# Sixteen 4 MB loads and sixteen 4 MB stores: two DMA queues, or one queue in a fixed order

## The reference

```python
W = weights[condition]                       # 64 x 128 x 128
return x + jnp.einsum('bct,bcd->bdt', x, W)  # 64 x 128 x 2048
```

## Time and profile before

| | us |
|---|---|
| median of 3 runs | 320.15 (319.94 to 320.36) |
| the profiled execution's own time | 320.04 |
| its span, first to last instruction | 318.3 |
| TensorE busy | 246.5 (77%) |
| VectorE busy | 146.8 (46%) |
| bytes moved | 135.29 MB, 425 GB/s over the span |

### The profile page before, as it was taken

The page is one execution under the profiler, slowest core; times in us unless marked ns, Lnnn a source line. Parts: engine busy times, 40 slices in busy tenths (PEclk is TensorE's granted clock), DMA queues, the critical chain, the costliest instruction groups (busy, mean ns, idle before and its releaser), DMA issues.

```text
span 318.3 us, 1351 instructions
## 1 busy us (share of the span) xinstructions
PE 246.5 (77%) x512; PEld 104.6 (33%) x512; DVE 146.8 (46%) x65; POOL 18.9 (6%) x69
## 2 busy tenths in 40 slices
PE   0099999991996979779398895939979596796960
PEld 0044444440442424334143342414424242342420
DVE  0026766762252553735237362641626556055460
POOL 0000000000010000001000010000000001000000
PEclk9999999998796998999779799996979999598996
DMA  8999999999999999999999999999999999999997
GB/s 329 416 441 457 371 424 457 397 461 399 457 424 432 449 408 461 412 445 432 424 453 404 457 424 432 445 412 461 399 457 424 432 449 408 461 395 461 420 411 298
DMA packets 5187, 135.29 MB, mean 425 GB/s; under 512 B 578, under 2 KB 578, under 8 KB 578
## 3 DMA queue, kind: packets, MB, share of 16 engines
q1 hardware_dynamic: 2448, 68.16, 50.0%
q10 hardware_dynamic: 2738, 67.11, 48.9%
HBM read 68.16 MB, written 67.11 MB: 425 GB/s over the span
## 4 chain that ended last, share of the span: by engine, by line
DMA 61%; PE 33%; DVE 3%; issue 0%; SPq 0%
PE product L92 33%; DMA out<-x_ring 32%; DMA x_ring<-x 30%; DVE x_ring L108 3%; SPq L58 0%
## 5 line engine op out<-in xcount | busy, mean ns | idle before, releaser
L92 PE MATMUL product<-x_ring,chosen_weights 128*128 128x512 f32 x512 | 246.5, 644 | 61.4 <-DMA x_ring<-x 61.4
L108 DVE TENSOR_TENSOR x_ring<-product,x_ring 128x2048 f32<-128x2048 f32 x64 | 146.7, 2291 | 161.4 <-PE product L92 161.4
L92 PEld LDWEIGHTS product<-x_ring,chosen_weights 128*128 128x128 f32 x512 | 104.6, 207 | 202.4 <-issue 122.7
L80 POOL COPY chosen_weights<-weight_table 128x128 f32 x64 | 18.7, 293 | 284.6 <-DVE x_ring L108 277.7
L102 DVE TENSOR_SCALAR state_row<-condition_row 1x64 int32<-1x64 int32 x1 | 0.2, 182 | 2.0 <-DMA condition_row<-condition 2.0
L137 POOL MEMSET const-float32-0.0<- 128x1 f32 x1 | 0.1, 98 | 0.1
L137 POOL MEMSET const-bfloat16-1.0<- 128x1 bf16 x1 | 0.1, 101 | 0.0
L137 POOL MEMSET const-uint8-127<- 128x1 uint8 x1 | 0.1, 101 | 0.0
L137 POOL MEMSET const-float32-1.0<- 128x1 f32 x1 | 0.1, 98 | 0.0
L137 POOL BASE_LOAD x1 | 0.0, 12 | 0.1
## 6 DMA issues: line engine op xcount, KB each, us to landing
x_ring<-x SPq DMA_DIRECT2D x16, 4096.0 KB, 26.7
out<-x_ring ACTq DMA_DIRECT2D x15, 4096.0 KB, 31.3
out<-x_ring ACTq DMA_DIRECT2D x4, 1024.0 KB, 9.1
weight_table<-weights SPq DMA_DIRECT2D x1, 1024.0 KB, 4.9
condition_row<-condition ACTq DMA_DIRECT2D x1, 0.2 KB
```

The source lines that it names most:

```text
L80: pool.tensor_copy(chosen_weights[b][:, :], weight_table[:, bass.ds(state[b] * features, features)]).then_inc(weights_chosen[b], 1)
L92: last = pe.matmul(product[:, b % psum_slots, m * BANK_COLUMNS:(m + 1) * BANK_COLUMNS], chosen_weights[b][:, :], x_ring[:, bass.ds(b * tim ...
L108: dve.tensor_tensor(tile, product[:, b % psum_slots, :], tile, AluOpType.add).then_inc(sum_done[b], 1)
```

## The change

All large transfers are issued by SP in one fixed order, and ACT keeps only the small load of `condition`. The order on SP: table; loads 0, 1, 2, 3; store 0; store 1, load 4; store 2, load 5; and so on to store 12, load 15; then stores 13, 14, 15. Ahead of each store SP waits for the last sum of the group; ahead of load g + 3 it waits for the landing of store g - 1. Group 15 is stored at once (4 MB). SP then waits for all stores.

```diff
         @block.sync
         def _(sp):
-            sp.dma_start(weight_table[:, :], weights.rearrange("c s d -> c (s d)")
-                          ).then_inc(table_loaded, 16)
-            for g in range(groups):
+            def load(g):
                 room = g % ROOMS
                 if g >= ROOMS:
                     sp.wait_ge(room_stored[room], 16 * (g // ROOMS))
                 sp.dma_start(x_ring[:, room * group_columns:(room + 1) * group_columns], x[g]
-                             ).then_inc(x_loaded[g % ROOMS], 16)
+                             ).then_inc(x_loaded[room], 16)
+            sp.dma_start(weight_table[:, :], weights.rearrange("c s d -> c (s d)")
+                          ).then_inc(table_loaded, 16)
+            for g in range(ROOMS):
+                load(g)
+            for g in range(groups):
+                room, last = g % ROOMS, (g % ROOMS + 1) * GROUP - 1
+                sp.wait_ge(sum_done[last], sums_wanted(g // ROOMS, last))
+                sp.dma_start(out[g], x_ring[:, room * group_columns:(room + 1) * group_columns]
+                             ).then_inc(room_stored[room], 16)
+                if 1 <= g <= groups - ROOMS:
+                    load(g - 1 + ROOMS)
+            for r in range(ROOMS):
+                sp.wait_ge(room_stored[r], 16 * (groups // ROOMS))
...
         def _(act):
...
-            for g in range(groups - 1):
-                room, last = g % ROOMS, (g % ROOMS + 1) * GROUP - 1
-                act.wait_ge(sum_done[last], sums_wanted(g // ROOMS, last))
-                act.dma_start(out[g], x_ring[:, room * group_columns:(room + 1) * group_columns]
-                              ).then_inc(room_stored[room], 16)
-            g = groups - 1
-            for i in range(GROUP):
-                b = (g % ROOMS) * GROUP + i
-                column = (g % ROOMS) * group_columns + i * time
-                act.wait_ge(sum_done[b], sums_wanted(g // ROOMS, b))
-                act.dma_start(out[g, :, i * time:(i + 1) * time], x_ring[:, column:column + time]
-                              ).then_inc(room_stored[g % ROOMS], 16)
```

2 lines of the change are left out of this document (removed).

## The result

The changed kernel takes 322.9 us, median of 6 runs (322.36 to 324.5), against 320.18 for the kernel before (319.94 to 320.36): ratio 1.0091, 95% interval 1.0073 to 1.011. It is slower by 0.9%, and these runs scatter over 2.1 us where those of the kernel before scatter over 0.4 (in the later runs the kernel before itself ranged from 319.90 to 321.78). I had forecast 319.2 and a range up to 321.3.

The account below looks back on a forecast made before the run. The DMA's rate, 9.68 us per 4 MB, was taken as the bound. Load 15's landing 286.4 + 0.4 + 0.1 + 15.7 + 2.3 + 12.2 + 0.4 + 1.74 gave 319.2 us, range 317.6 to 321.3.

Parts of the forecast that it names:

- What bounds it: Whole run: the DMA's rate sets the time, 9.68 us per 4 MB, loads, stores or mixed alike; TensorE does not.
- The waits on SP: Middle of the run: no wait on SP empties the queue, about 19 us of work lying ahead; cost 0.
- Stall and tail: DMA losses at the first stores (0 to 0.8 us, taken 0.4) and from lagging engines (0 to 1.4, taken 0).
- The stall, half of 0.8: DMA slowdown where first stores meet loads: 0 or 0.8 us depending on its origin, so 0.4 was taken.
- Store 15 alone, 12.2 us: End of the run: the last store meets a queue just run dry and pays 2.5 us over its bare time.
- TensorE's 15.7: TensorE's time for group 15 before the last store: 15.7 us, the middle of 14.0, 15.7 and 17.0.
- The last store is where the change pays and is paid: End: store 15 needs the whole group, the DMA idles some 1.5 us, about half of the 2.4 won is lost.
- the hole: Before store 15: the DMA was to stand still for about 1.5 us, waiting for the last group's sums.
- a turn of direction costs: Rival, chance 0.10: on one queue a store following a load may wait; 25 such places, 0.2 us each gives 324.0.
- The lag stays: Rival: single engines fall behind on long runs, load 15 lands 1.4 us late, 320.6; chance 0.15 including no change.
- the slow uncovered case: Rival, chance 0.17: the last group takes TensorE 17.0 us with the whole stall before its uncovered store, giving 320.9.

Follow-up runs that it names:

- stores alone: Changed kernel's one queue without computation, reordered to four loads, then 28 stores one behind the other: 318.99 us.
- with 13: Changed kernel with computation, loads and stores in pairs on the one queue, so 13 changes between loads and stores in place of 25: 321.92 us.
- with 48: Changed kernel's order without computation, each 4 MB transfer split in two, half stores and half loads alternating, about 48 changes of direction: 323.18 us.
- halves back to back: Changed kernel's order without computation, each 4 MB transfer issued as two of 2 MB in succession, 25 changes of direction: 324.97 us.
- three pieces: Kernel before, on its two queues, with the last group stored in pieces of 2, 1 and 1 MB instead of four of 1 MB: 320.18 us.

## Why the prediction was wrong

- **What bounds it**: right. The DMA's rate is the bound, one direction is as fast as the other (318.6 and 319.0 alone), and the changed kernel's rate in bulk stayed at 431 to 434.
- **The waits on SP**: right. Nothing in the middle ran dry (share 1.00 from 150 to 250); the cover of about 19 us held.
- **"Stall and tail ... I take 0"**: this is the step that failed. I priced the lag of single engines from load 2's landing, at a place where the queue had held nothing but loads, and carried it over to a queue that turns 25 times. Stores 0 to 11 came in 1.2 to 4.6 us late, and load 15 at 291.1 in place of the 286.8 (286.4 and half a stall) that the sum used. Without computation the same order lost 5.7 us against two queues. This one term is + 4.3 us.
- **The stall, half of 0.8**: it should have been whole, roughly 1 us. It comes with the first store, as stores alone show; what was missing of it is a part of the 4.3.
- **Store 15 alone, 12.2 us**: it took 11.2. I had read the start of the program as the start of any transfer. The Trainium skill, DMA: Bandwidth & Descriptors, section on the anatomy of one DMA, fits 2.0 us plus the bytes at 436 GB/s for transfers that GpSimd issues; by that an estimate of 11.6, which was the nearer. The measurement decides: 11.1 in the two-queue kernel with one last store, where no row began between 307 and the issue at 310.3. The changed kernel's 11.2 is partly another thing: store 14 had not landed when store 15 was issued. Term - 1.0.
- **TensorE's 15.7**: measured 15.48, - 0.2.

The terms give 319.2 + 4.3 - 1.0 - 0.2 = 322.3, and the profiled execution took 322.36.

- **"The last store is where the change pays and is paid"**: on two queues it costs 3.4 us. On the changed kernel's one queue undoing it gives nothing, since the slowest engine is late by just about the hole.
- **The rivals**: "a turn of direction costs" was given 0.10 and came nearest: the order in the queue makes the loss. I priced a pause of all engines at each turn; the runs show instead some engines falling behind, by a sum that is hardly larger with 25 turns than with 13 and no larger with 48. 4.3 us over 24 turns would be 0.18 each, but no such price fits all runs. "The lag stays" had the right look and a third of the size. My argument against the turns, that rows of both kinds alternate at 433 GB/s, was no argument: there each queue kept its direction. For the slow uncovered case I wrote that it decides from 17.3 us of TensorE without the stall; that is the figure with half of it, and without it 17.7 is right. It changes no chance.
- **The scatter**: 322.36 to 324.5, not forecast. The one-queue kernels without any TensorE work scatter as well (323.6 to 324.95, halves back to back 323.93 to 327.49), so TensorE's clock is not needed for it. Since two-queue kernels also have single late runs (321.78, and 322.4 with three pieces), I can't put it all down to the one queue.

What stays open: why an engine loses time in such a queue, which engines these are (the views give the sum of the 16), why the loss levels off, and how much of it belongs to the turns and how much to the thinner cover. The runs show that it goes with the order inside a queue, not with computation, and not with one queue as such.

## What to carry to other kernels

When the DMA is the bound, look at the spread of its engines and not at the mean share: a landing goes by the slowest of 16. Give loads and stores a queue each, and let the semaphores set the order; a fixed order on one queue looked better on paper and lost 5.7 us in the transfers alone. Price a thing from a stretch that has the feature in question, and cover the last store: one 4 MB piece in place of four cost 3.4 us of 320.

## What the runs showed of the hardware

- Loads and stores in turn on one queue, 25 turns, 32 transfers of 4 MB: 324.3 us, against 318.6 with each direction on its own queue and the same bytes. The Trainium skill, DMA: Bandwidth & Descriptors, section on issuing engines not being separate DMA queues, says that issuing from several engines saves only issue time, since all run on the same 16 engines. By that the two should be equal; here they differ by 5.7 us, with SP's issues of 0.34 us each hidden. Only with one direction in the one queue (318.6 and 319.0) were they nearly so. The measurement decides.
- The first stores of a run that follow a stretch of loads come with a gap of roughly 1 us in the DMA: 283 in place of 425 GB/s over 3.7 us on one queue, 262 in place of 434 over 2.0 us on two.
- A 4 MB store into an idle DMA landed 11.1 us after its issue, 1.4 over its bare 9.68 (two queues, one last store).
- Rows of 8 KB moved at 427 GB/s where rows of 32 KB moved at 433, and with loads alone at 423 where those of 32 KB moved at 434.
